# A three-layer graph network on one Trainium2 core: one gathered tile in forty is fetched row by row from SyncE

## The chip, the cores and the metric

The kernel runs on one core of one Trainium2 chip. The metric is the device time of one execution in microseconds (us). The kernel before takes 7026.36 us, the median of three runs (7025.17 to 7038.56). All data are float32.

## The reference

The input is a graph of 12,500 nodes with 128 features and 212,500 edges sorted by destination; each edge has a source, a destination, one of eight types and a weight. Two blocks follow each other:

```
# block 1 (called layer 0 in the kernel)
msg = relu((x[src] * edge_weight[:, None]) @ W_msg + b_msg)
x   = layernorm(x + relu(segment_sum(msg, dst) @ W_out + b_out))
# block 2: two relational layers (layers 1 and 2 in the kernel)
h   = x
for W, SW, b in ((w1, sl1, b1), (w2, sl2, b2)):
    xt  = einsum('nd,rde->rne', h, W)          # eight products for each node
    h   = relu(segment_sum(xt[type, src], dst) + h @ SW + b)
out = layernorm(x + h)
```

## The kernel before, in words

**Tables and gathers.** For each layer a table lies in DRAM: `msg_table` with one row of 128 floats (512 bytes) for each node, and `rel_tables[0]` and `rel_tables[1]` with eight rows for each node. The message of an edge is one row of a table, so the edge work of layers 1 and 2 is: fetch the rows that an index list names, and add them up by destination.

**Groups and tiles.** Edges are cut into 197 groups (`TRIMMED`) of 1079 edges; after edges that need no gather are taken out, a group fits in 1024 slots, which are 8 tiles (`TPG`) of 128 rows. For each tile GpSimd (POOL) issues one indirect DMA (`static_gather`, line 749) that brings 128 rows of 512 bytes into `rows`. `rows` is a ring of 8 groups (`RING`): the gathers of group n wait until TensorE has finished group n-8 (`edge_main.prod`). Layers 1 and 2 have 197 groups each, so 3152 gathers.

**The sum by destination.** VectorE builds one-hot matrices from the places of the edges (`dve_group`, line 816, two groups ahead in layers 1 and 2), ScalarE passes on that the rows have landed (`act_ready`, lines 719 and 720), TensorE multiplies each tile by its one-hot matrix and adds the eight tiles in PSUM (`pe_group`, line 869), and VectorE adds the result to a window of `agg` (`dve_add`, lines 852 and 857). The window's place is a register that `value_load` reads from SBUF.

**Nodes.** The nodes come in 98 blocks of 128. Their work is woven into the edge loop by `fused_loop`: a step has two halves, a half has one group, and a block is begun at the half that `half_of` names, two groups for one block. In layer 1 a block goes through feat (ACT), eight products (PE, line 1124), a copy and a pick of the node's own row (DVE, lines 1215, 1175 and 1186), and SyncE (SP) stores the block's part of the next table (`sync_nodes`, line 1278). In layer 2 SP loads the block of x (line 1271), the layer norm follows, and SP stores the output (line 1284). The instructions stand in each engine's queue in the order in which the Python loops emit them: on SP, the node transfers of a half, each behind a wait for the engine that makes its data.

**Between layers.** POOL begins a layer when all stores of the table have landed (`tables_ready`).

**Small transfers with an address from a register.** Layer 0 has some: in `sync_trim` SP reads a number from `base2` (`value_load`, lines 1738 and 1750) and writes 80 floats of one partition to a place of a line in DRAM which that number gives (lines 1740 and 1752). The code of one of them:

```
base = eng.value_load(base2[0:1, g:g + 1], min_val=0, max_val=N)
need(eng, s_line, 16 * g)
eng.dma_start(kind_line[bass.ds(base, MOST)].rearrange("(p n) -> p n", p=1),
              kinds[p:p + 1, c * MOST:(c + 1) * MOST]).then_inc(s_line, 16)
```

**Lists.** `rel_index` holds the row numbers of the gathers, [128, group, tile], made in layer 0 by `dve_unpack` in the steps `TURNS` (the last is 74). In layers 1 and 2 the one-hot matrices are in `deep`, so `onehot` is not used there.

Of the kernel before, what the change touches and what calls it, by code (L numbers as in the profile page):

```python
# [19 lines left out]
P = 128  # L20
F32 = mybir.dt.float32
I32 = mybir.dt.int32
ALU = mybir.AluOpType
ACT = mybir.ActivationFunctionType
AX = mybir.AxisListType.X
# [3 lines left out]
TPG = 8  # L29
HALF = TPG // 2  # L30
# [67 lines left out]
def build(nc, x, src, dst, edge_type, edge_weight, W_msg, b_msg, W_out, b_out,  # L98
# [30 lines left out]
    COUNT = (LAYER0, TRIMMED, TRIMMED)  # L129
    FIRST = (0, LAYER0, LAYER0 + TRIMMED)  # L130
    LAGS = (LAG, LAG_TRIM, LAG_TRIM)
    RD = R * D
    H = RD // 2

    ctx = ExitStack()
    with ctx:  # L136
# [63 lines left out]
        slots = [work[:, k * (ROW + 1):(k + 1) * (ROW + 1)] for k in (1, 2, 3, 4, 5, 0)]  # L200
        place2 = sb("place2", [P, HALVES * SIDE, TPG])
        picked = sb("picked", [P, RD])
        kind_of = sb("kind_of", [P, BLOCKS])
        weight_of = sb("weight_of", [P, BLOCKS - SELF_FROM])
        counted = sb("counted", [P, BLOCKS - SELF_FROM])
# [43 lines left out]
                   [bank[2], bank[3], bank[6], bank[7]]]  # L249
        ps_bm = bank[5][:, P:P + D]  # L250
        ps_own = ps_edge[0][:, P:2 * P]


        s_const = sem("s_const")
# [24 lines left out]
        s_quad = sem("s_quad")  # L279
        s_dealt = sem("s_dealt")  # L280
        s_start = sem("s_start")

        class NodeSems:
            def __init__(self, name, ln=False, table=False):
# [376 lines left out]
        def tiles_in(n, h):  # L661


            return min(HALF, max(REST_TILES - h * HALF, 0)) if n == RAW else HALF

        def act_index(layer, sems, step, lead, first):
# [193 lines left out]
        def pe_group(layer, sems, st):  # L860
            hot, total = hot_of(layer, st), sum_of(layer, st)
            for h in range(2):
                nc.tensor.wait_ge(sems.ready, st.n * 2 + (h + 1))
                tiles = HALF if st.late else tiles_in(st.n, h)
                most = TPG if st.late else tiles_in(st.n, 0) + tiles_in(st.n, 1)
                for j in range(tiles):
                    t = h * HALF + j
                    tile = rows[:, st.u, t, :]
                    ins = nc.tensor.matmul(total, tile,  # L869
                                           hot[:, t, :], start=t == 0, stop=t == most - 1)  # L870
            ins.then_inc(sems.prod, 1)
# [839 lines left out]
        def sync_trim(eng, step):  # L1711
# [42 lines left out]
            for b in KINDS_AT.get(step, ()):  # L1754
                r = TAIL if b == BLOCKS - 1 else P
                eng.wait_ge(s_line, 16 * min(2 * b + 5, TRIMMED))
                if b == 0:
# [3 lines left out]
                              kind_line[b * P:b * P + r].rearrange("(p n) -> p n", n=1)  # L1761
                              ).then_inc(s_kind, 16)

        def fused_edges(eng, layer, step, q):


            first, groups = FIRST[layer], COUNT[layer]
            g = step * PAIR + q

            def table_of(g):  # L1770


                if layer:
                    return 0, place2, base2
                return (0, place, base_row) if g < TAKEN else (SIDE - TAKEN, place2, base2)

            def group(g):
                return Block(g, first, first + g, RING) if g < groups else None

            st = group(g)  # L1780
            if eng is nc.gpsimd:
                if st is not None and (layer or g >= EARLY):
                    static_gather(layer, g)
            elif eng is nc.vector:
                ahead = AHEAD if layer else 0
                for a in range(0 if g == 0 else ahead, ahead + 1):
                    if group(g + a) is not None:
                        lead, spots, _ = table_of(g + a)
                        dve_group(layer, edge_main, group(g + a), lead, spots)
                if layer == 0 and not q and step:  # L1790
                    dve_trim(step - 1)
                if 0 < g <= groups:
                    lead, _, bases = table_of(g - 1)
                    dve_add(layer, edge_main, group(g - 1), lead, bases)
                if layer == 0 and q and step in TURNS:
                    dve_unpack(step)
                if layer == 0 and q and step in WEIGHT_TURNS:
                    dve_weights(step)
            elif st is None:
                if eng is nc.tensor and layer == 0:  # L1800
                    pe_own_message(g)
                return
            elif eng is nc.tensor:
                if layer == 0 and g == 0:
                    pe_convert(0)
                if layer == 0 and g + 1 < EARLY:
                    pe_convert(g + 1)
                if layer == 0 and q and step in TURN_ORDER:
                    pe_trim(step)
                if layer == 0:  # L1810
                    pe_own_message(g)
                pe_group(layer, edge_main, st)
            elif eng is nc.scalar:
                if layer == 0 and g == 0:
                    act_convert(0)
                if layer == 0 and g + 1 < EARLY:
                    act_convert(g + 1)
                if layer == 0 or g == 0:
                    act_ready(layer, edge_main, st)
                if layer and group(g + 1) is not None:  # L1820
                    act_ready(layer, edge_main, group(g + 1))

        def fused_loop(eng, layer):
# [4 lines left out]
            for s in range(steps):  # L1828
                for q in range(PAIR):
                    fused_edges(eng, layer, s, q)  # L1830
                    node_step(eng, layer, half_stage(layer, s * PAIR + q), True)
                if layer == 0 and eng is nc.sync:
                    sync_trim(eng, s)
# [192 lines left out]
```

## Time and profile before

| | |
|---|---|
| median of 3 runs | 7026.36 us |
| span of the profiled execution, first to last instruction | 6065.7 us |
| median less span | 960.7 us |
| the profiled execution's own time | not printed by the profile beyond its span |
| POOL busy | 4511.3 us (74%) |
| PE, DVE, ACT busy | 2683.3, 2607.2, 1031.7 us |
| DMA engines busy, mean | 0.2 to 0.3 of the time |
| layer 1, first to last gather | 2101.11 to 4067.70 us |
| layer 2, first to last gather | 4087.45 to 6053.44 us |

Busy time counts only the operations themselves. POOL's busy time leaves out some 0.30 us between two gathers, which the profile calls issue. SP has no busy time in the page: its instructions are issues of DMAs, register instructions and loads of registers, which are read from the views by line. Times in these views are in ns.

### The profile page before, as it was taken

The numbers are of one execution on the slowest core, as the hardware profiler recorded it, in microseconds if no ns is written. First come the engines' busy times: TensorE is split into PE (matmuls) and PEld (weight loads), VectorE is DVE, ScalarE is ACT, GpSimd is POOL, SyncE is SP. The second block draws the span as 40 slices with busy tenths as digits, with TensorE's granted clock in tenths as the row PEclk, the third lists the DMA queues.
The fourth block names the chain that finished last, engine by engine and source line by source line (L and its number), as shares of the span: only waits on it lengthen the run. The fifth ranks groups of instructions, "written<-read, shape, count | busy, mean of one in ns | idle before, by whom it ended". The sixth has DMA issues, their size and how long they took to land.

```text
span 6065.7 us, 46678 instructions
## 1 busy us (share of the span) xinstructions
PE 2683.3 (44%) x11862; PEld 2109.9 (35%) x11862; DVE 2607.2 (43%) x4881; ACT 1031.7 (17%) x2878; POOL 4511.3 (74%) x4794
## 2 busy tenths in 40 slices
PE   6244555555555544444444444443333333333333
PEld 5233444444444332332323323233333333333333
DVE  6888888777555523333333333331222222222221
ACT  3333444444444300000000000000000000000000
POOL 7767777777777577777777777767777777777777
PEclk8666677766667666666666666665555555555555
DMA  6222323333233222222222222222222222222221
GB/s 182 61 86 80 99 89 100 92 91 91 86 92 89 81 70 80 81 77 81 77 81 80 77 81 77 81 79 57 59 60 60 59 60 59 60 59 59 60 59 57
DMA packets 279550, 471.55 MB, mean 78 GB/s; under 512 B 110125, under 2 KB 169385, under 8 KB 279270
## 3 DMA queue, kind: packets, MB, share of 16 engines
q0 software_dynamic: 152672, 312.98, 18.5%
q1 hardware_dynamic: 125446, 155.09, 7.4%
q8 instruction: 96, 1.57, 0.1%
q14 instruction: 184, 1.51, 0.1%
q10 hardware_dynamic: 1152, 0.39, 0.0%
HBM read 346.02 MB, written 122.09 MB: 77 GB/s over the span
## 4 chain that ended last, share of the span: by engine, by line
POOL 49%; issue 16%; PE 0%; DMA 0%; DVE 0%; POOLq 0%; ACT 0%; DVEq 0%; ACTq 0%; SPq 0%
POOL rows L749 49%; PE bank L1124 0%; POOLq L626 0%; DMA rows<-rel_table,rel_index 0%; PE bank L869 0%; DMA rel_table<-tab 0%; DVE picked L1175 0%; DMA rows<-msg_table,msg_index 0%; DVE tab L1215 0%; ACT tab L1056 0%; PE bank L1138 0%; ACT rows L697 0%; POOLq L136 0%; DVE stats L1242 0%; DVE y L1238 0%
## 5 line engine op out<-in xcount | busy, mean ns | idle before, releaser
L749 POOL DMA_INDIRECT rows<-rel_table,rel_index x3152 | 2973.8, 943 | 1010.7 <-issue 960.6
L749 POOL DMA_INDIRECT rows<-msg_table,msg_index x1555 | 1470.0, 945 | 508.5 <-issue 472.4
L869 PE MATMUL bank<-work,rows 128*128 128x128 f32 x6304 | 1149.7, 352 | 675.8 <-ACTq L720 675.8
L869 PEld LDWEIGHTS bank<-work,rows 128*128 128x128 f32 x6304 | 1079.6, 262 | 813.9 <-ACTq L720 752.0
L869 PE MATMUL bank<-onehot,rows 128*128 128x128 f32 x3238 | 673.8, 384 | 938.3 <-ACT rows L715 914.9
L1124 PE MATMUL bank<-wr,feat 128*128 128x512 f32 x784 | 627.1, 946 | 908.7 <-ACT feat L1082 892.2
L869 PEld LDWEIGHTS bank<-onehot,rows 128*128 128x128 f32 x3238 | 606.5, 283 | 1047.5 <-ACT rows L715 1011.3
L697 ACT ACTIVATE rows<-rows,weight 128x128 f32<-128x128 f32 x1555 | 494.8, 389 | 800.1 <-DVE onehot L816 484.4
L1124 PEld LDWEIGHTS bank<-wr,feat 128*128 128x128 f32 x784 | 216.7, 306 | 1113.5 <-ACT feat L1082 913.4
L1175 DVE TENSOR_TENSOR picked<-bank,chosen 128x512 f32<-128x512 f32 x392 | 265.3, 689 | 740.1 <-ACT tab L1056 733.3
L816 DVE TENSOR_TENSOR work<-bank,place 128x1024 f32<-128x1024 f32 x394 | 476.7, 1211 | 7.4 <-ACT agg L1034 3.7
L1238 DVE SCALAR_TENSOR_TENSOR y<-bank,xin 128x128 f32<-128x128 f32 x196 | 57.0, 291 | 813.0 <-PE bank L1112 809.6
L1215 DVE COPY tab<-bank 128x512 f32<-128x512 f32 x196 | 134.6, 687 | 629.2 <-PE bank L1124 629.2
L1112 PE MATMUL bank<-ident,sums 128*128 128x128 f32 x98 | 46.5, 474 | 803.8 <-ACT sums L1086 803.8
L833 DVE TENSOR_TENSOR rows<-rows,bank 128x512 f32<-128x512 f32 x389 | 265.2, 682 | 263.7 <-ACT rows L697 263.0
L1186 DVE TENSOR_REDUCE place<-picked 128x128 f32<-128x1024 f32 x196 | 368.2, 1878 | 19.3 <-DVE picked L1175 0.5
L1112 PEld LDWEIGHTS bank<-ident,sums 128*128 128x128 f32 x98 | 17.9, 183 | 832.4 <-ACT sums L1086 832.4
L857 DVE TENSOR_TENSOR agg<-agg,bank 128x128 f32 x597 | 169.7, 284 | 293.5 <-PE bank L869 227.5
L1056 ACT ACTIVATE tab<-bank 128x512 f32<-128x512 f32 x196 | 114.9, 586 | 933.1 <-DMA rows<-rel_table,rel_index 920.7
L1094 ACT ACTIVATE std<-mv,eps 128x1 f32<-128x1 f32 x196 | 57.3, 292 | 1247.8 <-DMA rows<-rel_table,rel_index 930.2
L1205 DVE RECIPROCAL rstd<-std 128x1 f32<-128x1 f32 x196 | 31.3, 160 | 550.4 <-ACT std L1094 550.0
L715 ACT ACTIVATE rows<-rows 128x512 f32<-128x512 f32 x405 | 247.8, 614 | 4.9 <-DVEq L830 3.7
(145 smaller groups left out, 1798.8 us busy)
## 6 DMA issues: line engine op xcount, KB each, us to landing
rel_table<-tab SPq DMA_DIRECT2D x196, 512.0 KB, 3.0
rows<-rel_table,rel_index POOLq DMA_INDIRECT x3152, 2.5
rows<-msg_table,msg_index POOLq DMA_INDIRECT x1555, 2.5
x_dram<-normed SPq DMA_DIRECT2D x98, 64.0 KB, 3.0
xin<-x_dram SPq DMA_DIRECT2D x98, 64.0 KB, 1.9
xin<-in_x_dram SPq DMA_DIRECT2D x97, 64.0 KB
out_dram<-normed SPq DMA_DIRECT2D x97, 64.0 KB, 1.6
tab<-in_x_dram SPq DMA_DIRECT2D x24, 256.0 KB, 4.6
```

What stands on the lines that cost most here:

```text
L697: ins = nc.scalar.activation(tile, tile, ACT.Copy, scale=weight[:, g, t:t + 1])
L715: nc.scalar.activation(v, v, ACT.Relu).then_inc(sems.ready, 1)
L749: nc.gpsimd.indirect_dma_start(rows[:, u, t, :], None, table, bass.IndirectOffsetOnAxis(ap=table_index[:, g, t:t + 1], axis=0)).then_inc(e ...
L816: nc.vector.tensor_tensor(out=hot_of(layer, st), in0=ps_columns.unsqueeze(1).to_broadcast([P, TPG, P]), in1=group_cols(spots, st, lead).re ...
L833: nc.vector.tensor_tensor(out=v, in0=v, in1=ps_bm.unsqueeze(1).to_broadcast([P, HALF, D]), op=ALU.add).then_inc(sems.scaled, 1)
L857: nc.vector.tensor_tensor(out=window, in0=window, in1=sum_of(layer, st), op=ALU.add).then_inc(sems.added, 1)
L869: ins = nc.tensor.matmul(total, tile, hot[:, t, :], start=t == 0, stop=t == most - 1)
L1056: nc.scalar.activation(tab[:, st.u, H:RD], ps_tab[1][:, :], ACT.Copy).then_inc(sems.taba, 1)
L1124: nc.tensor.matmul(ps_tab[h][:, :], feat[:, st.u, :], wr[layer][:, h * H:(h + 1) * H], start=True, stop=True).then_inc(sems.prod, 1)
L1175: v.tensor_tensor(out=picked[:, h * H:(h + 1) * H].rearrange("p (r e) -> p r e", r=R // 2), in0=ps_tab[h][:, :].rearrange("p (r e) -> p r ...
L1186: nc.vector.tensor_reduce(out=own_row_of(st.b), in_=picked[:, :].rearrange("p (r e) -> p e r", r=R), axis=AX, op=ALU.add).then_inc(sems.pi ...
L1215: nc.vector.tensor_copy(tab[:, st.u, 0:H], ps_tab[0][:, :]).then_inc(sems.tabd, 1)
```

## The change

In layers 1 and 2 the last tile of the groups 4, 9, ..., 194 (39 of 197 in each layer) is no longer gathered by POOL. SP fetches its 128 rows one by one, each with a DMA of its own of 512 bytes, into one of four buffers in `onehot`. The row numbers are turned once, in layer 0, into a list of byte offsets in SBUF, `fetch_list` (one copy on DVE, one transpose on PE, one multiplication on DVE, steps 76 and 77). SP loads sixteen of the offsets at a time into registers. Fetch j is spread over five halves, a fifth of its pieces in each, ahead of the node transfers of that half: half h has a fifth of the fetch h // 5 + 1, which belongs to group 5 (h // 5) + 9. At half 0 the whole of fetch 0 stands ahead of it, and before this the wait for the table.

```
@@ build
+    FETCH_EVERY = 5
+    FETCH_GROUPS = range(FETCH_EVERY - 1, TRIMMED, FETCH_EVERY)
+    FETCHES = len(FETCH_GROUPS)
+    FETCH_RING = 4
+    FETCHED = {FIRST[layer] + g: (layer - 1) * FETCHES + j
+               for layer in (1, 2) for j, g in enumerate(FETCH_GROUPS)}
...
+        fetch_list = sb("fetch_list", [FETCHES, P], I32)
+        fetch_index = sb("fetch_index", [P, FETCHES])
+        fetched_rows = onehot[:, 0, 0:FETCH_RING, :]
@@ tiles_in
+            if n in FETCHED:
+                return HALF - h
@@ pe_group
-                tiles = HALF if st.late else tiles_in(st.n, h)
-                most = TPG if st.late else tiles_in(st.n, 0) + tiles_in(st.n, 1)
+                full = st.late or layer
+                tiles = HALF if full else tiles_in(st.n, h)
+                most = TPG if full else tiles_in(st.n, 0) + tiles_in(st.n, 1)
...
+                    if t == TPG - 1 and not st.late and st.n in FETCHED:
+                        k = FETCHED[st.n]
+                        nc.tensor.wait_ge(s_fetched[k % FETCH_RING],
+                                          16 * P * (k // FETCH_RING + 1))
+                        tile = fetched_rows[:, k % FETCH_RING, :]
@@ new functions
+        LIST_STEP = TURN_ORDER[-1] + 2
+        def dve_fetch_index():
+            nc.vector.wait_ge(s_unpacked, len(TURNS))
+            nc.vector.tensor_copy(fetch_index[:, :],
+                                  rel_index[:, FETCH_EVERY - 1:TRIMMED:FETCH_EVERY, TPG - 1]
+                                  ).then_inc(s_fetch_index, 1)
+        def pe_fetch_list():
+            nc.tensor.wait_ge(s_fetch_index, 1)
+            nc.tensor.wait_ge(edge_main.added, (LIST_STEP + 1) * PAIR)
+            nc.tensor.transpose(ps_fetch, fetch_index[:, :], ident[:, :]
+                                ).then_inc(s_fetch_turned, 1)
+            nc.tensor.wait_ge(s_fetch_list, 1)
+        def dve_fetch_list():
+            nc.vector.wait_ge(s_fetch_turned, 1)
+            nc.vector.tensor_scalar(fetch_list[:, :], ps_fetch, float(4 * D), None, ALU.mult
+                                    ).then_inc(s_fetch_list, 1)
+        LOADED = 16
+        def sync_fetch(eng, layer, half):
+            parts = [(half // FETCH_EVERY + 1, half % FETCH_EVERY)]
+            if half == 0:
+                eng.wait_ge(s_fetch_list, 1)
+                eng.wait_ge(edge_main.prod, FIRST[1])
+                parts = [(0, k) for k in range(FETCH_EVERY)] + parts
+            pieces = P // LOADED
+            table = rel_tables[layer - 1].rearrange("n d -> (n d)").bitcast(U8)
+            for j, part in parts:
+                if j >= FETCHES:
+                    continue
+                k = (layer - 1) * FETCHES + j
+                if part == 0 and k >= FETCH_RING:
+                    free = next(n for n in FETCHED if FETCHED[n] == k - FETCH_RING)
+                    eng.wait_ge(edge_main.prod, free + 1)
+                for c in range(pieces * part // FETCH_EVERY, pieces * (part + 1) // FETCH_EVERY):
+                    _, at = nc.values_load_multi_w_load_instructions(
+                        fetch_list[j:j + 1, c * LOADED:(c + 1) * LOADED],
+                        engines=[mybir.EngineType.SP], min_val=0,
+                        max_val=(NP * R - 1) * 4 * D,
+                        skip_runtime_bounds_check_because="indices of the edges are below N * R")
+                    for i in range(LOADED):
+                        p = c * LOADED + i
+                        eng.dma_start(
+                            fetched_rows[p:p + 1, k % FETCH_RING, :].bitcast(U8),
+                            table[bass.ds(at[i], 4 * D)].rearrange("(p n) -> p n", p=1)
+                            ).then_inc(s_fetched[k % FETCH_RING], 16)
@@ fused_loop
+                    if layer and eng is nc.sync:
+                        if s + q == 0:
+                            tables_ready(eng, layer)
+                        sync_fetch(eng, layer, s * PAIR + q)
                     node_step(eng, layer, half_stage(layer, s * PAIR + q), True)
```

`fused_edges` calls the functions for the list in layer 0.

## Rows read from the trace of the kernel before

**Rows 1.** The page: span, busy time, and the DMA engines' share.

```profile
span 6065.7 us, 46678 instructions
PE 2683.3 (44%) x11862; PEld 2109.9 (35%) x11862; DVE 2607.2 (43%) x4881; ACT 1031.7 (17%) x2878; POOL 4511.3 (74%) x4794
DMA  6222323333233222222222222222222222222221
```

**Rows 2.** Line 749, POOL's gathers: count, ns min/median/max, what its waits were for.

```profile
L749 POOL DMA_INDIRECT rows<-rel_table,rel_index x3152: 939/944/962, 2101.1 to 6053.4; - x197
  issue: 1451.9, 4740
  DMA rel_table<-tab: 50.1, 2
  PE bank L869: 36.1, 27
```

**Rows 3.** Timeline of POOL at the two turns between layers: start us, us, instruction.

```profile
2101.11 0.94 POOL L749 DMA_INDIRECT rows<-rel_table,rel_index  x1 [31.29 <-DMA rel_table<-tab]
...
4067.70 0.94 POOL L749 DMA_INDIRECT rows<-rel_table,rel_index  x1 [0.30 <-issue]
4087.45 0.94 POOL L749 DMA_INDIRECT rows<-rel_table,rel_index  x1 [18.80 <-DMA rel_table<-tab]
4088.70 0.94 POOL L749 DMA_INDIRECT rows<-rel_table,rel_index  x1 [0.31 <-issue]
```

**Rows 4.** The chain that ended last, its final steps: start us, us, step.

```profile
6053.44 3.01 DMA rows<-rel_table,rel_index
6056.54 2.09 PE bank L869 x8
```

**Rows 5.** Busy time by engine (PE, PEld, DVE, ACT, POOL), layers 1 and 2.

```profile
2101.00:4070.00 1969.00, 840.99 (x3764) 587.07 (x3763) 660.09 (x870) 100.15 (x215) 1486.89 (x1576) 0.67 0.25 78
4087.00:6055.00 1968.00, 732.06 (x3244) 653.01 (x3242) 399.78 (x871) 58.09 (x192) 1486.96 (x1576) 0.55 0.21 59
```

**Rows 6.** SP's own waits: line, for whom, us in total, times, longest.

```profile
SPq L1276 <- ACT tab L1056: 2990.9, 188, 75.5
SPq L1284 <- DVE normed L1208: 2059.0, 100, 164.6
```

**Rows 7.** Lines 1752 and 1750 at 282 to 286 us, four in close order.

```profile
L1752 SPq ALU_OP  x4: 33/33/33, 282.0 to 285.7; - x4
L1752 SPq MOVE kind_line<-weight x4: 38/38/38, 282.1 to 285.8; - x4
L1752 SPq DMA_DIRECT2D kind_line<-weight x4: 257/258/258, 282.2 to 285.9; - x4
...
L1750 SPq TENSOR_LOAD <-msg_index x3: 475/480/482, 282.5 to 284.9; - x3
L1750 SPq FUSED_REGOPS  x3: 147/147/147, 283.0 to 285.4; - x3
L1750 SPq SEQ_ASSERT  x3: 18/18/18, 283.2 to 285.6; - x3
```

**Rows 8.** The same two lines, at 1510 to 1515 us.

```profile
L1752 SPq DMA_DIRECT2D kind_line<-weight x2: 291/294/297, 1511.4 to 1512.9; - x2
...
L1750 SPq TENSOR_LOAD <-msg_index x2: 492/776/1060, 1509.9 to 1511.7; - x2
```

**Rows 9.** Line 381: a transfer of one partition with a fixed address, on SP.

```profile
L381 SPq DMA_DIRECT2D rows<-in_dst_dram x1: 253/253/253, 8.4 to 8.4; - x1
```

**Rows 10.** Line 852, DVE's loads of one register.

```profile
L852 DVEq TENSOR_LOAD <-msg_index x492: 298/306/1030, 1115.4 to 6057.2; - x164
```

**Rows 11.** SP's node transfers in layers 1 and 2: lines 1278, 1284 and 1271.

```profile
L1278 SPq DMA_DIRECT2D rel_table<-tab x196: 332/333/377, 287.2 to 4083.9; - x196
...
L1284 SPq DMA_DIRECT2D out_dram<-normed x98: 332/344/344, 4159.6 to 6062.9; - x98
...
L1271 SPq DMA_DIRECT2D xin<-x_dram x98: 340/432/1368, 4084.4 to 6017.4; - x98
```

**Rows 12.** The page: SP's queue, packets, MB, share of 16 engines.

```profile
q1 hardware_dynamic: 125446, 155.09, 7.4%
```

More of the change, by code:

```diff
@@ L22 @@
 I32 = mybir.dt.int32
+U8 = mybir.dt.uint8
 ALU = mybir.AluOpType
@@ L251, in build @@
         ps_own = ps_edge[0][:, P:2 * P]
+        ps_fetch = ps_edge[1][0:FETCHES, 2 * P:3 * P]
         s_const = sem("s_const")
@@ L281, in build @@
         s_start = sem("s_start")
+        s_fetch_index, s_fetch_turned, s_fetch_list = s_quads, s_part, s_partuse
+        s_fetched = [s_blank, s_blanked, s_member, s_ranked]
         class NodeSems:
@@ L1798, in fused_edges @@
                     dve_weights(step)
+                if layer == 0 and q and step == LIST_STEP:
+                    dve_fetch_index()
+                if layer == 0 and q and step == LIST_STEP + 1:
+                    dve_fetch_list()
             elif st is None:
@@ L1809, in fused_edges @@
                     pe_trim(step)
+                if layer == 0 and q and step == LIST_STEP + 1:
+                    pe_fetch_list()
                 if layer == 0:
```

## The prediction

> **What bounds the kernel now.** I read the page first (span, busy time), then POOL's gathers by line, the timeline of POOL at the turns between layers, busy time by stretch, and last SP's own waits and SP's instructions by line. The page gives a span of 6065.7 us in which POOL is the busiest engine, 4511.3 us, and the DMA engines are busy 0.2 to 0.3 of the time [rows 1]. The 3152 gathers of layers 1 and 2 take 944 ns each; in the whole kernel POOL waited for TensorE only 36.1 us and for tables 50.1 us, the rest is its own issue [rows 2]. From 2101.11 to 4067.70 us POOL issues 1576 gathers without a hole, so one costs (4067.70 - 2101.11) / 1575 = 1.249 us, a group of eight 9.99 us [rows 3]. PE is busy 841 of these 1969 us, DVE 660 [rows 5]. POOL's queue is the bound of both layers. After the last gather come 3.0 us of landing and 2.1 us of matmuls [rows 4], and the nodes' end; the next layer's first gather is 19.75 us after the last one [rows 3]. SP does nearly nothing: 2990.9 and 2059.0 us waiting for the nodes [rows 6].
>
> The sum is made on the span. The profile prints no time for its execution beyond the span; the median of the runs is 7026.36, 960.7 us more. I carry these 960.7 us over unchanged.
>
> **What is removed.** 39 gathers in each layer, 78 x 1.249 = 97.4 us of POOL. Five groups then cost POOL 39 x 1.249 = 48.7 us instead of 49.95. If all else hides, that is the gain.
>
> **What is added on SP: one row.** A fetch has 128 DMAs of one partition with an address from a register, 8 loads of sixteen registers, and SP has 48.7 us for it. The nearest rows are the four small writes at 282 to 286 us [rows 7]: TENSOR_LOAD 480, FUSED_REGOPS 147, SEQ_ASSERT 18, ALU_OP 33, MOVE 38, DMA 257, together 973 ns, while they start every (285.9 - 282.2) / 3 = 1.23 us. So six gaps take 0.26 us, 0.043 each. The new row has a byte offset, so I take the ALU_OP (the multiplication of the offset by four) as gone; the check (FUSED_REGOPS, SEQ_ASSERT) is switched off in the code. MOVE carries the DMA's own name in the trace, so I keep it. A row is 38 + 257 + 2 x 43 = 0.381 us. Bounds: below, the DMA alone, 257 + 43 = 0.300 us (a fixed address takes 253 [rows 9]); above, two register instructions as now, 33 + 38 + 257 + 3 x 43 = 0.457 us. I take 0.381, because only the multiplication has lost its reason. 128 x 0.381 = 48.8 us. After a load the first two DMAs are slower, 291 and 297 ns instead of 257 [rows 8]: 8 x (0.034 + 0.040) = 0.6 us.
>
> **The loads.** The trace has only loads of one register: 480 ns in close order, 1060 when it had been idle [rows 7, 8], 306 on DVE [rows 10]. Sixteen words in one instruction cost at least the 0.48 + 0.043 = 0.52 us of one and at most sixteen of them, 8.4 us. I take the slow row, 1.06 + 0.04 = 1.10 us: some growth with the words, most of a load being its fixed part. 8 x 1.10 = 8.8 us.
>
> One page speaks against this. The Trainium skill, "Runtime: NRT & Kernel Launch", section "Instruction fetch mechanics", says that register loads (from HBM) take about 200 ns a register even in bulk. That would be 3.2 us for sixteen, an estimate from the page's figure, 8 x 2.1 = 16.8 us more in each fetch, and the time 1310 us above my forecast. No row here has a load of more than one word, so nothing here settles it.
>
> **SP's other work.** In five groups there are 2.5 blocks: in layer 1 a table store, 2.5 x (0.333 + 0.04) = 0.9 us; in layer 2 an output and a load, 2.5 x (0.344 + 0.432 + 0.08) = 2.1 us [rows 11].
>
> **The sum.** A fetch costs SP 48.8 + 0.6 + 8.8 + 0.9 = 59.1 us in layer 1 and 60.3 in layer 2. POOL needs 48.7. SP is then the slower queue by over 10 us in each five groups, and becomes the bound. The wait moves: TensorE stops before the last tile of groups 4, 9, ...; behind this wait stand that group's end, the next groups and the nodes' products, and for them wait DVE, ACT and, through `edge_main.prod`, POOL, whose ring of 8 groups fills up. SP's waits for the nodes become empty: at half h it waits for group h-1 and issues rows for a group five to nine further on, so once it is late nothing holds it. Between fetches TensorE finds the gathered tiles ready and does the five groups in a run, and its total work fits easily [rows 5].
>
> Layer 1 begins for SP with POOL's first gather, 2101.1, behind the same wait for the table. The 39 fetches end 39 x 59.1 = 2305 us later. Then follow a landing (3.0), groups 194 to 196 (3 x 2.1) [rows 4], whose gathers are long there, and the turn, 19.75 less the landing and the 2.1 that are in it: 2305 + 25 = 2330 us instead of 4087.45 - 2101.11 = 1986. Layer 2: 39 x 60.3 = 2352, and 18 us of end (9.3, and 6065.7 - 6056.54 - 2.09 = 7.1, with 2 for a node block that is late) = 2370 us instead of 1978. The differences are +344 and +392, together +736. Span 6802, time 7762 us; I say 7760.
>
> **Edits with nothing in the sum.** The list in layer 0 (two small DVE operations, one PE transpose, two waits of PE): PE has behind it an own message and a group; POOL is eight groups ahead and its queue sets the layer. Uncovered it would cost 1 to 3 us, once. One matmul per fetched group reads another buffer: same size. The wait on the ring of four buffers is for a group twenty groups back. SP's table stores now stand behind up to ten us of rows, but the last stores of a layer come when the fetches are over. The program has 78 x (128 x 2 + 8) = 20,600 more instructions; if the 960.7 us outside the span grew with the 46,678 traced ones, that would be up to 20.6 ns x 20,600 = 424 us. I take 0, since no row ties the two together.
>
> **The rivals.**
>
> Two register instructions stay for each row (a copy of the offset, and the MOVE). For it: every such DMA in the trace has two [rows 7]. Against: only one of them is named with the DMA, and the other's work is gone. 128 x 0.076 = 9.7 us more in each fetch, x 78 = +760: 8520.
>
> Loads cost by the word. For it: a short load takes 0.3 on DVE, so a word's round trip may be most of it [rows 10]. Against: the spread from 0.30 to 1.06 shows a large part that isn't the word. At 0.25 us a word a load is 4.0 us, 8 x 2.9 = 23 us more, x 78 = +1800: 9560.
>
> Faster: rows and loads hide behind the gathers. Its place is SP's queue, its price the period of a fetch, and it decides at 48.7 us: below that, POOL stays the bound. With no register instruction, 128 x 0.300 = 38.4, and short loads, 8 x 0.52 = 4.2, a fetch is 44.1 us in layer 1, 45.3 in layer 2. The first fetch is late for group 4, but POOL's ring takes that up. Time 7026 - 97 = 6930. For it: one transfer's data is nothing, 0.074 x 16 x 6065.7 / 125446 = 57 ns a packet [rows 12]. Against: MOVE stands in each such DMA.
>
> The Trainium skill, "DMA: Bandwidth & Descriptors", section "Issuing engines are not separate DMA queues", has a rule on this side: the sequencer's time to start a DMA is usually small beside the DMA itself. By it the rows would hide and this rival's 6930 would hold. The trace disagrees for rows this small: 257 ns of issue [rows 7] against 57 ns of packet.
>
> No visible change: a period near 50 us, which needs row and loads between the two cases: 7026.
>
> The rows of a fetch land one after another. The four writes each waited for the landing of the one before and still started every 1.23 us [rows 7]. If a row cost this, a fetch would be 157 us and the time 7760 + 78 x 98 = 15,400. It needs each landing to wait for the last, for which nothing speaks.
>
> **Numbers.** Forecast 0.43 (7760, its own range 7400 to 8200: loads of 0.52 us take off 78 x 4.6 = 360, of 1.8 us add 440). Two register instructions 0.28 (8520). Loads by the word 0.10. Landing in turn 0.03. Faster 0.14 (6930). No change 0.02. The range reaches from 6900, which takes in the faster case, to 8700; what is left out is the load case and the landing case, 0.13, and the upper edge of the second. A change of 0.2%, 14 us, is what can be told from none. Faster 0.14, same 0.02, slower 0.84.
>
> **What would show it.** On SP, 9984 row DMAs of about 257 ns, one MOVE each, no ALU_OP; 624 loads of about 1.1 us; starts of rows 0.38 us apart; SP's waits for the nodes in layers 1 and 2 near zero. On PE, waits at line 869 of tens of us each, about 39 in a layer. POOL with waits for PE of some 700 us in all. Layer 1 some 2330 us. It would be wrong if SP still waited thousands of us for nodes, if POOL still issued without holes, or if the difference lay outside the span.

## The result and the profile after

| | time, us |
|---|---|
| before | 7032.46 (median of 4, 7025.17 to 7039.81) |
| changed | 9115.27 (median of 4, 9101.42 to 9120.61) |
| ratio | 1.2957, 95% interval 1.2942 to 1.2973 |

The changed kernel is 30% slower; the forecast was 7760, 10% slower, with a range up to 8700. One thing has to be said ahead of all else: both kernels run at two paces, and all runs of one set, made together on one chip, have the same one. Before takes 6064 to 6071 us on the chips numbered 0 and 6 and 7022 to 7090 on 3, 4 and 7. The trace of before that stands ahead of the prediction (span 6065.7) was taken at the quick pace, while the runs were made at the slow one. Rows of before at the slow pace come from a later trace (`c2_before`, span 7033.0), and times are compared within one pace.

The page of the changed kernel, whose own time was 9101.42 us: span, busy times, and the chain of waits.

```profile
span 9099.7 us, 67204 instructions
PE 2537.1 (28%) x11863; PEld 2050.4 (23%) x11863; DVE 2592.6 (28%) x4883; ACT 1036.3 (11%) x2878; POOL 4435.5 (49%) x4716
...
SPq 47%; issue 29%; DVE 12%; another core or an unknown queue 6%; ACT 3%; PE 2%; DMA 1%; DVEq 1%; POOL 0%; ACTq 0%; POOLq 0%
SPq L1836 38%; SPq L1829 8%; ACT rows L714 2%; DVE onehot L833 2%; DVE place L1209 1%; DVE rows L850 1%; DVE picked L1198 1%; PE bank L892 1%; DVE bank L1576 1%; DVE work L1577 1%; DVE work L1580 1%; DVE bank L1569 1%; DVE tab L1238 1%; DMA onehot<-rel_table 1%
```

POOL's share of the span is 49%; before has 74% at the quick pace [rows 1] and 64% at the slow one. The chain runs through SP: 38% through the row DMAs, 8% through the loads. SP's lines 1836 (a row) and 1829 (a load of sixteen), ns min/median/max, first and last start in us, and who waited:

```profile
L1836 SPq MOVE onehot<-rel_table x9984: 1/29/1407, 2490.5 to 9085.2; - x200
L1836 SPq DMA_DIRECT2D onehot<-rel_table x9984: 1/228/1407, 2490.6 to 9085.2; - x200
...
  PE bank L892: 2934.3, 78
...
L1829 SPq TENSOR_LOAD <-fetch_list x624: 2/1242/2257, 2489.3 to 9078.7; - x156
```

All 78 fetches are waited for by TensorE, 2934 us in all. The median row costs 29 + 228 ns, less than forecast, but single instructions of SP take up to 1.4 us, even a MOVE. Without the 21 us of the turn between the layers a fetch takes (9085.2 - 2490.5 - 21) / 78 = 84.3 us. POOL's waits, to be held against [rows 2]:

```profile
L766 POOL DMA_INDIRECT rows<-rel_table,rel_index x3074: 938/944/989, 2490.1 to 9000.0; - x193
...
  PE bank L892: 2263.5, 121
  issue: 1459.3, 4382
  remote: 640.0, 182
```

The wait for TensorE is 2263.5 us; in before it is 36.1 at the quick pace and 261.4 at the slow one. SP's own waits, before at the slow pace and then the changed kernel:

```profile
SPq L1276 <- ACT tab L1056: 2061.5, 108, 138.9
SPq L1284 <- DVE normed L1208: 1257.3, 43, 138.5
```
```profile
SPq L1299 <- ACT tab L1079: 461.2, 44, 26.1
SPq L1307 <- DVE normed L1231: 213.5, 4, 205.9
```

What is left is nearly all in layer 0: from 2490 us on the two waits of the changed kernel are 13.6 and 7.6 us, those of before 1660.6 and 1257.3.

And layer 0, which the change hardly touches, ends 389 us later: the first gather of layer 1 is at 2490.1, not 2101.11 [rows 3]. That is the pace, as the next section shows.

### The profile page after: what moved, and what is told of

It is laid out like the page before. It is cut to its first block, busy times and chain, and to the rows that moved or that the text cites. A ratio compares the mean times of both kernels' runs of the same rounds, so it can differ in the third digit from the quotient of the medians.

```text
span 9099.7 us, 67204 instructions
## 1 busy us (share of the span) xinstructions
PE 2537.1 (28%) x11863; PEld 2050.4 (23%) x11863; DVE 2592.6 (28%) x4883; ACT 1036.3 (11%) x2878; POOL 4435.5 (49%) x4716
## 4 chain that ended last, share of the span: by engine, by line
SPq 47%; issue 29%; DVE 12%; another core or an unknown queue 6%; ACT 3%; PE 2%; DMA 1%; DVEq 1%; POOL 0%; ACTq 0%; POOLq 0%
SPq L1836 38%; SPq L1829 8%; ACT rows L714 2%; DVE onehot L833 2%; DVE place L1209 1%; DVE rows L850 1%; DVE picked L1198 1%; PE bank L892 1%; DVE bank L1576 1%; DVE work L1577 1%; DVE work L1580 1%; DVE bank L1569 1%; DVE tab L1238 1%; DMA onehot<-rel_table 1%
## 5 line engine op out<-in xcount | busy, mean ns | idle before, releaser
L766 POOL DMA_INDIRECT rows<-rel_table,rel_index x3074 | 2899.9, 943 | 3677.8 <-PE bank L892 2133.8
L892 PE MATMUL bank<-work,rows 128*128 128x128 f32 x6148 | 1009.6, 333 | 264.3 <-issue 254.9
L892 PEld LDWEIGHTS bank<-work,rows 128*128 128x128 f32 x6148 | 992.3, 251 | 333.2 <-issue 321.7
L892 PE MATMUL bank<-onehot,rows 128*128 128x128 f32 x3238 | 650.2, 378 | 994.0 <-issue 540.8
L892 PE MATMUL bank<-work,onehot 128*128 128x128 f32 x156 | 62.1, 501 | 2934.3 <-DMA onehot<-rel_table 2934.3
L1147 PE MATMUL bank<-wr,feat 128*128 128x512 f32 x784 | 585.2, 889 | 551.0 <-ACT feat L1105 338.7
L892 PEld LDWEIGHTS bank<-work,onehot 128*128 128x128 f32 x156 | 39.1, 311 | 2955.1 <-DMA onehot<-rel_table 2955.1
```

What stands on the lines that cost most here:

```text
L766: nc.gpsimd.indirect_dma_start(rows[:, u, t, :], None, table, bass.IndirectOffsetOnAxis(ap=table_index[:, g, t:t + 1], axis=0)).then_inc(e ...
L892: ins = nc.tensor.matmul(total, tile, hot[:, t, :], start=t == 0, stop=t == most - 1)
L1147: nc.tensor.matmul(ps_tab[h][:, :], feat[:, st.u, :], wr[layer][:, h * H:(h + 1) * H], start=True, stop=True).then_inc(sems.prod, 1)
```

## Experiments

### The kernel before, for its own time beside its trace

No edit. Expected:

> The kernel before, unchanged, to see its trace beside its own time. The changed kernel's span (9099.7 us) is 2 us below its time (9101.42), while the trace of before had a span 960 us below the median. Theory A: that trace was of a quicker execution than the timed ones; then this run has a span near 7025 us, layer 0 lasts some 400 us longer than the 2069 us of the first trace, and POOL has holes at the ends of groups, as it has in layer 0 of the changed kernel. Theory B: 960 us lie outside the span and the change alone slowed layer 0 by 390 us; then the span is near 6066 us again and layer 0 ends near 2069 us.

Measured: 6063.84 us, span 6062.1. This chip had the quick pace, where neither theory can be told from the other; the run only showed that time and span differ by 2 us. On another chip:

> The kernel before, for a trace at the slow pace if this chip has it (7030 to 7081 us; the quick one gives 6064 again and tells nothing new). Theory I (at the slow pace every queue is held up now and then for some 0.7 us, more the more instructions and transfers run): the layer-0 part lasts 2400 to 2450 us as in the changed kernel, and POOL's gathers of layers 1 and 2 have holes too, with each layer near 2250 us. Theory A' (only SP's rows suffer): layers 1 and 2 at 1986 us each and all the difference in layer 0.

Measured: 7034.74 us, span 7033.0. Its line of gathers:

```profile
L749 POOL DMA_INDIRECT rows<-rel_table,rel_index x3152: 942/947/990, 2490.5 to 7013.7; - x197
...
  issue: 1418.9, 4539
  remote: 692.1, 161
  PE bank L869: 261.4, 63
```

A gather takes what it took (947 against 944 ns), but POOL waits 692 us for something that the profile can't name ("remote" on a kernel of one core) and 261 us for TensorE. Layer 1 starts at 2490.5, as in the changed kernel, and its gathers take 2251 us instead of 1967; both are what theory I expected. So nothing of the 960 us lay outside the span: the first trace showed another execution than the timed ones. That the DMA engines or the clock are what is slower there falls by the same pages: a packet of SP's queue takes 7.4% x 16 x 6065.7 / 125446 = 57 ns at the quick pace [rows 12] and 6.5% x 16 x 7033.0 / 125446 = 58 ns here, and the mean granted clock of TensorE is 0.634 here and 0.646 in the quick control, 2% apart where the times are 16% apart. SP is held up too, in a line that at the quick pace is nearly constant. First the slow pace, then the same two groups in the first trace:

```profile
L1752 SPq MOVE kind_line<-weight x197: 1/38/712, 350.0 to 2393.4; - x197
L1752 SPq DMA_DIRECT2D kind_line<-weight x197: 2/290/1395, 351.4 to 2394.7; - x197
```
```profile
L1752 SPq MOVE kind_line<-weight x197: 37/38/42, 279.1 to 1991.4; - x197
L1752 SPq DMA_DIRECT2D kind_line<-weight x197: 253/291/332, 279.1 to 1991.4; - x197
```

### The change at both paces

No edit. Expected of the first repeat:

> The changed kernel again, beside the kernel before on the same chip. Both kernels have now been seen at two paces: before at 7032 and 6067 us, and where it ran at 6067 SP's row DMAs started every 0.32 us without any stall (in the kernel with every tenth group). Theory A (SP is the bound, nothing else): a fetch costs 128 x 0.322 + 8 x 1.29 = 51.5 us and some 1 to 2 us of node transfers, against 48.7 for POOL; where before takes 6067, 39 x 53 = 2067 + 25 and 2085 + 18 us for the two layers, in all 6295 us, ratio 1.04. Theory C (the rows and the gathers hold each other up whenever SP never rests): the ratio is again near 1.30, 7850 us where before takes 6067, with rows at 0.57 us as a mean. If before takes 7030 here, the changed kernel takes 9100 by both.

It met the slow pace: 9217.23 us against 7081.47, ratio 1.3008 (1.2986 to 1.3029). Expected of the second:

> The changed kernel once more. Where before takes 7081 us, it has now been measured twice at 1.30. Where before takes 6067 us it has not run. Theory A (SP's queue is the bound; the stalls are a matter of the slow pace alone): at the quick pace 6295 us, ratio 1.04, rows 0.322 us apart without stalls, a fetch about 53 us. Theory C (stalls come at either pace once SP never rests): at the quick pace 7850 us, ratio 1.30.

Measured at the quick pace: 6456.68 us against 6068.01, ratio 1.064 (1.0618 to 1.0661). So the loss at the pace without stalls is 6.4%; neither 4% nor 30%. Theory C, stalls at either pace, falls; theory A is right in kind and 162 us too low, 2.1 us a fetch. SP's lines at the quick pace:

```profile
L1836 SPq MOVE onehot<-rel_table x9984: 29/29/38, 2098.4 to 6442.1; - x200
L1836 SPq DMA_DIRECT2D onehot<-rel_table x9984: 227/228/394, 2098.5 to 6442.2; - x200
...
  PE bank L892: 2151.6, 78
...
L1829 SPq TENSOR_LOAD <-fetch_list x624: 1141/1255/2298, 2097.2 to 6435.6; - x156
```

No row is held up. SP's timeline at the quick and then at the slow pace (start, us, instruction, count):

```profile
3016.76 24.97 SPq L1836 DMA_DIRECT2D onehot<-rel_table  x64
3041.83 0.37 SPq L1301 DMA_DIRECT2D rel_table<-tab  x1
3044.43 15.59 SPq L1836 DMA_DIRECT2D onehot<-rel_table  x39
```
```profile
3018.36 33.72 SPq L1836 DMA_DIRECT2D onehot<-rel_table  x48
3052.18 0.38 SPq L1301 DMA_DIRECT2D rel_table<-tab  x1
```

64 rows with three loads between them take 24.97 us: 64 x 0.322 + 3 x 1.27 = 24.4, and some for the first two rows after a load. 48 rows with two loads at the slow pace take 33.72, where 18.0 were due. After a table store the next row starts 2.60 us later, since the load between them is slow. That is so behind the table stores of layer 1 only: the 92 loads that stand right behind one take 1.87 to 2.30 us, the 92 behind an output store of layer 2 take 1.15 to 1.32, and those behind rows 1.16 to 1.46. By layer:

```profile
L1829 SPq TENSOR_LOAD <-fetch_list x312: 1155/1267/2298, 2097.2 to 4271.6; - x156
L1829 SPq TENSOR_LOAD <-fetch_list x312: 1141/1245/1421, 4297.4 to 6435.6; - x156
```

A fetch of layer 1 is 128 x 0.322 = 41.2 us, 8 x 1.27 = 10.2, and for each of its 92 / 39 = 2.4 table stores 0.42 and 0.83 of slow load, 2.9; together 54.3, measured 55.9. Layer 2 has 2.2 us of loads and stores for the nodes in place of the 2.9: 53.6, measured 55.0. Of the missing 1.5 us the trace shows 1.0 in rows above 0.322, the first after each load among them. Over both layers it is (6442.1 - 2098.4 - 21) / 78 = 55.4.

The stalls of the slow pace come in stretches. SP's row instructions from 3019 to 3036 us, and from 3037 to 3067:

```profile
L1836 SPq MOVE onehot<-rel_table x8: 3/690/702, 3019.7 to 3035.8; - x8
L1836 SPq DMA_DIRECT2D onehot<-rel_table x7: 691/697/708, 3021.1 to 3035.1; - x7
```
```profile
L1836 SPq DMA_DIRECT2D onehot<-rel_table x70: 227/228/272, 3036.9 to 3065.9; - x70
L1836 SPq MOVE onehot<-rel_table x69: 29/29/38, 3037.2 to 3065.9; - x69
```

In the first stretch POOL issues gathers, untouched themselves (10.4 of 17 us busy), and the starts and ends of SP's instructions are some 0.7 us apart. In the second POOL rests, waiting for TensorE, and SP has its quick pace back. Counted over the two layers, the next row starts 0.91 us later as a mean while POOL issues gathers (one began in the 1.3 us before) and 0.47 while it rests, loads between rows included; at the quick pace it is 0.43 and 0.45.

### Fewer fetches

```
-    FETCH_EVERY = 5
+    FETCH_EVERY = 6        # in other kernels 10 and 15
```

> Every tenth group's last tile in place of every fifth: 19 fetches in a layer, POOL has 79 x 1.25 = 98.7 us between two. If SP is the bound with 83 us a fetch, as the changed kernel shows, it now fits: time 7032 - 38 x 1.25 = 6985 us, 0.7% below before. If rows are held up by the gathers beside them (theory D) a fetch may take 100 us, since POOL then never rests: time 7050 to 7200 us. If the slowdown has another cause than SP's queue, such as the wait on TensorE by itself, half the fetches give half the loss: near 8070 us.

Measured at the quick pace: 6020.07 against 6067.02 us, ratio 0.9922 (0.9905 to 0.9938); the expected saving was 47.5 us, the measured one 47.0.

> Every sixth group's last tile: 32 fetches a layer, POOL has 47 x 1.249 = 58.7 us between two. Theory A: 51.5 + 2 = 53.5 us of SP fit, all is hidden, and 64 gathers of 1.249 us are saved: 6067 - 80 = 5987 us. Theory C: SP never rests here for long either, rows stall, the kernel is slower than before.

This met the slow pace: 8513.22 against 7081.47, ratio 1.2023 (1.2003 to 1.2043), with TensorE waiting 1962.6 us for the 64 fetches. Again:

> Every sixth group. At the quick pace by theory A: 51.5 + 2 us of SP fit into 58.7, so 6067 - 64 x 1.249 = 5987 us. By theory C: slower than before. At the slow pace 8513 us was measured, and should come again.

Measured at the quick pace: 5987.4 against 6068.01 us, ratio 0.9868 (0.9851 to 0.9884). It is faster than before by 80.6 us, the 64 x 1.249 = 80 us of its 64 gathers. POOL's line shows its queue without new holes:

```profile
L766 POOL DMA_INDIRECT rows<-rel_table,rel_index x3088: 939/944/970, 2099.1 to 5972.4; - x193
...
  issue: 1421.2, 4639
...
  PE bank L892: 46.5, 65
```

With every sixth group POOL needs 47 x 1.249 = 58.7 us between two fetches and SP some 56: hidden. With every fifth 48.7 against 55: lost. That fits the point which the prediction gave for its rival "faster", a fetch as long as POOL's work between two of them.

### Parts of a fetch alone

Rows from fixed addresses, without loads and MOVE (other rows than the reference's are fetched):

```
-                    _, at = nc.values_load_multi_w_load_instructions(
...
-                            table[bass.ds(at[i], 4 * D)].rearrange("(p n) -> p n", p=1)
+                            table[p * 4 * D * R:(p * R + 1) * 4 * D].rearrange("(p n) -> p n", p=1)
```

> The 128 row DMAs of each fetch stay, but from fixed addresses: no loads of registers and no MOVE (the rows fetched are wrong ones). In the changed kernel a row starts 0.32 us after the last one as a median, but 0.57 us as a mean, and a fetch takes 83 us. Theory D (the DMAs themselves are held up while POOL's gathers run): the mean of a row stays near 0.5 us, a fetch takes 60 to 70 us, the time is near 8100 us. Theory I (the stalls come with the number of SP's instructions, their supply or their recording): with half the instructions the stalls halve, a row costs near 0.35 us, a fetch 45 us, and the time falls to that of before or below, 7000 us.

> Row DMAs from fixed addresses, no loads, no MOVE, as before. At the quick pace 5972 us again. At the slow pace, theory D: the rows stall as in the changed kernel (0.57 us as a mean), a fetch near 70 us, time near 8500 us. Theory I: half the instructions, so half the stalls, a fetch near 50 us, time near 7100 us.

5972.28 and 5971.65 us at the quick pace: 128 rows, 0.295 us apart in close order, are 37.8 us and fit behind the gathers; 94.7 and 96.4 us are saved of the 97.4 us of 78 gathers.

No row DMA, four semaphore increments in place of each. The trace has no register loads on line 1829 either, though the expectation counts on them; nothing uses their values any more:

```
-                        eng.dma_start(
...
-                            ).then_inc(s_fetched[k % FETCH_RING], 16)
+                        for _ in range(4):
+                            eng.sem_inc(s_fetched[k % FETCH_RING], 4)
```

> The loads of sixteen registers stay, but each row DMA is replaced by four increments of the semaphore it would raise (no row is fetched). SP has more instructions than in the changed kernel (512 short ones in place of 256 for each fetch) and no row DMA. Theory D (the DMAs are what is held up): no instruction takes 0.7 us, SP needs 8 x 1.3 + 512 x 0.05 = 36 us a fetch, POOL is the bound and the time is near 6930 us. Theory I (the number of instructions): stalls of 0.7 us in these too, SP well above 50 us a fetch, time above 7100 us.

> Row DMAs replaced by four semaphore increments each (no row is fetched), as before. At the quick pace 5968 us again. At the slow pace it tells what stalls SP: theory D (the row DMAs, beside POOL's gathers): no stalls of 0.7 us on SP, time some 7000 us, below before's 7081. Theory I (whatever holds up instructions there goes by their number): 512 instructions a fetch in place of 256, SP stalls on them, time above 9217 us.

5967.77 and 5968.83 us at the quick pace, hidden too (512 increments, 0.059 us apart in close order, are 30.2 us). Then both at the slow pace, beside 7036.99 us for before:

> Row DMAs from fixed addresses, no loads and no MOVE. Quick pace: 5972 us. Slow pace: theory D: rows at 0.57 us or more as a mean, time near 8500 us. Theory I: half the instructions, time near 7100 to 7500 us.

> Four semaphore increments in place of each row DMA (no row is fetched). Quick pace: 5968 us for the third time. Slow pace: theory D (the row DMAs beside the gathers are held up): no stalls on SP, time below before's. Theory I (the number of instructions): twice the instructions of the changed kernel on SP, stalls of 0.7 us among them, time above 8000 us.

Measured 7739.62 us for the fixed rows and 8594.94 for the increments. The lines (a row; an increment):

```profile
L1831 SPq DMA_DIRECT2D onehot<-rel_table x9984: 1/252/1462, 2489.7 to 7722.8; - x200
```
```profile
L1837 SPq EVENT_SEMAPHORE  x39387: 1/17/2128, 2486.5 to 8579.4; - x200
...
  PE bank L892: 2195.8, 78
```

The kernel without any row DMA is the slower one: an increment of 17 ns comes every (8579.4 - 2486.5) / 39387 = 0.155 us as a mean. Theory D, that it is SP's DMAs that are held up, falls. Theory I holds for the increments (above 8000 us expected) and misses for the fixed rows (7100 to 7500 expected), so the number of instructions alone doesn't give the loss: 128 row DMAs cost 67 us a fetch, 512 increments 78, 264 instructions of the changed kernel 84. That is some 27, 46 and 29 us above what the same work needs at the quick pace.

What theory D had right is the place. Increments from 3208 to 3236 us, with 22 gathers of POOL beside them, and from 3237 to 3265, with one:

```profile
L1837 SPq EVENT_SEMAPHORE  x66: 1/17/1401, 3208.0 to 3234.9; - x66
```
```profile
L1837 SPq EVENT_SEMAPHORE  x373: 3/17/708, 3236.3 to 3265.0; - x187
```

Counted over the two layers, an increment comes every 0.335 us while POOL issues gathers and every 0.078 while it rests; beside the gathers at the quick pace it is 0.065. So at the slow pace any instruction of SP is held up, and mostly beside POOL's gathers. TensorE, VectorE and ScalarE make little difference: beside gathers alone it is 0.35, with all of them 0.27.

### The costs that were disputed

Eight offsets in a load (`LOADED = 8`):

> Eight offsets in each load, so 16 loads for a fetch; all else as in the changed kernel. It tells the fixed part of a load from its part for each word. If a load of 16 (1.25 us) is nearly all fixed, a fetch is 8 x 1.3 = 10 us longer: 6295 + 78 x 10 = 7080 us. If it goes by the word, from a fixed 0.43 (one word takes 0.48), eight words take 0.84 us and 16 loads 13.9 us instead of 10.3: +3.6 us a fetch, 6580 us.

It met the slow pace: 9404.28 us against 7081.47, 187 above the changed kernel there. The load's median is the useful number, since a median is hardly touched by the pace (1237 ns for sixteen words beside it, 1255 at the quick one):

```profile
L1829 SPq TENSOR_LOAD <-fetch_list x1248: 1/784/1557, 2504.6 to 9383.2; - x179
```

One word takes 480 ns [rows 7], eight 784, sixteen 1250: 0.04 to 0.06 us for each further word. The times that were expected are for the quick pace and can't be judged.

Offsets in words in place of bytes:

```
-            nc.vector.tensor_scalar(fetch_list[:, :], ps_fetch, float(4 * D), None, ALU.mult
+            nc.vector.tensor_scalar(fetch_list[:, :], ps_fetch, float(D), None, ALU.mult
...
-            table = rel_tables[layer - 1].rearrange("n d -> (n d)").bitcast(U8)
+            table = rel_tables[layer - 1].rearrange("n d -> (n d)")
...
-                            table[bass.ds(at[i], 4 * D)].rearrange("(p n) -> p n", p=1)
+                            table[bass.ds(at[i], D)].rearrange("(p n) -> p n", p=1)
```

> Offsets in float32 words instead of bytes (the multiplication by four comes back). If it costs one more register instruction a row, as in the small writes of layer 0 (ALU_OP 33 ns and a gap of 0.03 to 0.04), a row is 0.38 to 0.40 us, a fetch 8 to 10 us longer, and the time 6295 + 78 x 9 = 7000 us. If the ALU_OP is hidden behind the DMA before it, no change: 6295 us.

10247.27 us at the slow pace, 1030 above the changed kernel. The multiplication is back as one instruction a row:

```profile
L1836 SPq ALU_OP  x9984: 1/33/1424, 2511.4 to 10230.0; - x200
L1836 SPq MOVE onehot<-rel_table x9984: 1/29/1423, 2511.5 to 10230.1; - x200
```

So the byte offsets take away the ALU_OP and leave the MOVE, as the forecast had it. 9984 instructions of 33 ns cost 1030 us there, 0.103 us each; what they cost at the quick pace wasn't measured.

### Few fetches at the slow pace

> Every tenth group. Quick pace: 6020 us again, 0.992. Slow pace: POOL takes some 112 us for its 79 gathers there, by the ratio 7050 to 6067, and a fetch 83 to 90 us where POOL rests part of the time; if rows stall beside gathers at 0.9 us each (the mean in the changed kernel while POOL is busy) a fetch is 128 x 0.9 = 115 us, so 1.00 to 1.03.

Measured: 7095.57 against 7036.99 us, ratio 1.0086 (1.0057 to 1.0115), within what was expected.

> Every fifteenth group's last tile: 13 fetches in a layer, 26 gathers saved, to find a version that is faster at both paces. SP has 119 gathers' time between two fetches. Quick pace (119 x 1.249 = 148.6 us): all hidden, 6067 - 26 x 1.249 = 6035 us, 0.995. Slow pace: a fetch took 118 us with every tenth group, and POOL needs about 119 x 1.43 = 170 us; it fits, so 7035 - 26 x 1.43 = 6998 us, 0.995, if SP's added instructions don't slow POOL's own queue. If they do (every tenth group gave 1.009 where its fetch of 118 us and POOL's 113 to 118 were close), the gain is eaten: 1.00.

Measured: 7051.87 against 7032.36 us, ratio 1.0026 (1.0017 to 1.0035), so the saving of 0.5% did not come and the second case, "the gain is eaten", did. In the kernel with every tenth group TensorE waited for fetched rows only once:

```profile
L1836 SPq DMA_DIRECT2D onehot<-rel_table x4864: 1/228/1424, 2485.1 to 7032.4; - x195
...
  PE bank L892: 23.6, 1
```
```profile
L766 POOL DMA_INDIRECT rows<-rel_table,rel_index x3114: 938/944/1008, 2484.5 to 7073.4; - x195
...
  issue: 1379.2, 4413
  remote: 752.7, 219
  PE bank L892: 341.6, 91
```

Its fetches are hidden and it has 38 gathers fewer, yet POOL waits 61 us longer for what has no name and 80 us longer for TensorE than in before at this pace. Those counts are for the whole kernel, and they fit what the times say: at the slow pace the added work costs the other queues more than the gathers save, even where SP has room. None of the kernels that give the reference's result is faster there.

## Why the prediction was wrong

**The step that failed.** The prediction has: "the median of the runs is 7026.36, 960.7 us more. I carry these 960.7 us over unchanged." They were not around the span but in it: time less span is 2 us in the changed kernel and in both traced controls. All terms were read from an execution at the quick pace and added to a time of the slow one, so a fetch was put at 59.1 and 60.3 us, and at the slow pace it takes 84.3. Before needs 57.0 us there for five groups (layers of 2251.3 and 2243.4 us, each 39.4 times five groups); 78 x 27.3 = 2130 us, and 2083 are measured. The forecast had 736 us. At the quick pace the same kernel loses 6456.8 - 6065.7 = 391. The slow pace's loss is outside the range because none of the rivals had stalls in SP.

**The bound and where it goes: right.** SP takes POOL's place, TensorE waits at the last tile, POOL's ring fills, and SP's waits empty out; each was found where the text said. TensorE has 78 waits for fetched rows, 39 in a layer. POOL's wait for TensorE at the quick pace is 411 us, and not some 700, in proportion to the smaller loss.

**A row: mis-sized, right in kind.** Forecast 0.381 us, measured 0.322: MOVE 29 ns (38 in the small writes), DMA 228 (257), and gaps of 0.03 where 0.043 had been taken as a mean over other instructions. The small writes went the other way (from SBUF to DRAM), had 320 bytes and other instructions between them; which of these makes them dearer isn't shown. 128 x 0.059 = 7.6 us a fetch too much.

**Loads: mis-sized, and one row misread.** A load of sixteen words was taken as 1.10 us with its gap and is 1.27: 1.4 us a fetch too little. The price came from the load of 1060 ns in [rows 8], read as that of a queue "when it had been idle". SP's timeline of before shows that it wasn't idle: that load, which starts at 1509.9, stands right behind two node transfers, the first of them a table store:

```profile
1509.03 0.35 SPq L1278 DMA_DIRECT2D rel_table<-tab  x1
1509.42 0.43 SPq L1284 DMA_DIRECT2D x_dram<-normed  x1
```

So 1060 ns is one word behind these stores, and that it comes near the 1250 of sixteen words in close order is luck. For the same reason the sum had no term for sixteen words behind a table store: 2.0 us too little in layer 1, nothing in layer 2. The rule of about 200 ns a register ("Runtime: NRT & Kernel Launch" of the Trainium skill, "Instruction fetch mechanics", for loads from HBM) would have made 3.2 us of sixteen words, an estimate; the trace has 1.25 for these loads from SBUF.

**The sum.** 59.1 and 60.3 us forecast, 55.9 and 55.0 measured at the quick pace. The difference is to be taken from before's 49.95 us for five groups: some 9.8 us were forecast, 5.5 measured, hence 391 us in place of 736. An error of 7% in the fetch is one of 44% in a difference of two near numbers.

**The rivals.** "Two register instructions" is refuted by the trace (one MOVE), "loads by the word" at 0.25 us a word by the loads of eight and sixteen, "landing in turn" by rows 0.322 us apart. "Faster" is what happens as soon as a fetch fits, as the kernels with every sixth and tenth group show at the quick pace. The rule that starting a DMA is small beside the DMA ("DMA: Bandwidth & Descriptors" of the Trainium skill, "Issuing engines are not separate DMA queues") doesn't carry over to rows of 512 bytes: 0.322 us of issue each, one behind another, against 57 ns of packet [rows 12].

**The list in layer 0, the outside of the span.** No gather is later for the list (2097.9 against 2101.1 us for the first one of layer 1 at the quick pace), and the 20,500 additional instructions add nothing around the span.

**What stays open.** What the slow pace is. Shown is: it goes with the chip or with the time at which its runs were made, since each of the five numbered chips came up once; at that pace SP's instructions of any kind are held up, in steps of 0.7 us and mostly beside POOL's gathers; POOL's queue has holes though a gather takes the same time; and the cost grows with what SP issues, whether or not this is DMA. One rival no run tests is that the recording itself makes the slow pace. The trace of before holds 100,764 semaphore events at the quick pace (`c0_before`) and 23,033 at the slow one, for the same program, which fits that part of POOL's waits has no releaser there. Held-up instructions show a start or an end each 0.7 us, and durations of 1 to 3 ns among them, as if their records came out one by one. Every run whose span is listed was recorded, and no execution without records is there to be set against them. So it isn't shown that the 30%, or the 960 us of before, would be there without the profiler.

## What to carry to other kernels

Before a sum is made, hold the profile's span against the time that it is to explain: here a gap of 14% meant that the trace showed another execution, and no term of it can be carried over before the gap has a place. Work moved to an idle queue has to fit between two of its deadlines, so count its instructions, loads included, against that period and leave a margin: here 55 us into 58.7 gave -1.3%, into 48.7 gave +6.4%, both at the quick pace. And before a row is taken as a price, look at what stands ahead of it in its queue. A change that adds thousands of small instructions on one queue should be timed on more than one chip.

## What the runs showed of the hardware that was not expected

- The same program, recorded, ran at 6064 to 6071 us on two chips and at 7022 to 7090 on three others, with the same 944 to 947 ns for a gather.
- At the slow pace a semaphore increment of 17 ns, repeated without pause, came every 0.335 us beside POOL's gathers and every 0.078 while POOL rested; at the quick pace every 0.059 in close order.
- A load of registers on SP costs 0.48 us for one word, 0.78 for eight, 1.25 for sixteen. Right behind a store of a table block (512 KB) sixteen words took 1.87 to 2.30 us, behind a store of 64 KB they took 1.15 to 1.32.
- A DMA of one 512-byte row in close order takes 228 ns of SP with its address in a register and 252 with a fixed one.
